# Mixer of a token tower: parameter products woven between the projection jobs, end values turned earlier, B's copies shared differently

## The reference, cut to what matters

```python
proj = x @ w_in
gate, vraw, params = jnp.split(proj, [D_INNER, 2 * D_INNER], axis=-1)
v = jax.nn.silu(conv)                      # causal convolution of vraw over 4 tokens
bc = (v @ w_bc).reshape(Bsz, T, N_HEADS, 2, D_STATE)
Bm = _l2norm(bc[..., 0, :]); Cm = _l2norm(bc[..., 1, :])
A = jax.nn.softplus(p[..., 0]); dt = jax.nn.sigmoid(p[..., 1])
S = 1.0 / (1.0 + dt * dt * A)
...
z = s * (z - d * a * xs + d * bu)          # one token's step, for each head
xs = xs + d * z
y = jnp.einsum('bhn,bhnp->bhp', Ct, xs)
```

## Time and profile before

| what | us |
| --- | --- |
| median of 3 runs | 1756.95 (1753.33 to 1761.33) |
| the profiled execution, its own time | 1750.74 |
| its span from first to last instruction | 1748.9 |
| `mixer_project`, from its first work | 332.3 to 402.3 |
| `mixer_responses` | 402.3 to 449.9 |
| `mixer_bc` | 449.9 to 477.6 |
| `mixer_chain` | 477.6 to 576.9 |

### The profile page before, as it was taken

One profiled execution on the slowest core, in us unless ns is written; L12 is line 12 of the kernel. 1 busy time (PEld: TensorE's weight loads), 2 busy tenths in 40 slices (PEclk: granted clock), 3 DMA queues, 4 the chain that ended last, 5 costly groups with the idle time before them and its releaser, 6 DMA issues. The chain is left out here.

```text
span 1748.9 us, 36641 instructions
## 1 busy us (share of the span) xinstructions
PE 1476.3 (84%) x14396; PEld 1114.7 (64%) x14396; DVE 1280.7 (73%) x2547; ACT 1048.4 (60%) x1871; POOL 414.7 (24%) x424
## 2 busy tenths in 40 slices
PE   5889998798499889899999719995697999999795
PEld 5889897697455657654445618895676744446574
DVE  5988897489789547369995757884655389994566
ACT  6998897334678264548896306664002549995565
POOL 0000000101656120359910117872001310000200
PEclk9999999699599989879999659998797979999897
DMA  5110100100000100025500732121100000000101
GB/s 146 28 42 29 37 1 20 36 1 1 7 2 2 35 1 15 1 82 170 171 16 2 210 119 61 61 62 50 48 1 14 1 1 2 2 2 2 35 1 37
DMA packets 52748, 67.96 MB, mean 39 GB/s; under 512 B 11535, under 2 KB 41489, under 8 KB 52578
## 3 DMA queue, kind: packets, MB, share of 16 engines
q1 hardware_dynamic: 46022, 50.30, 9.6%
q0 software_dynamic: 3840, 9.18, 1.8%
q10 hardware_dynamic: 2716, 6.14, 1.4%
HBM read 46.97 MB, written 18.65 MB: 38 GB/s over the span
## 5 line engine op out<-in xcount | busy, mean ns | idle before, releaser
L2068 DVE TENSOR_REDUCE att_max<-banks 104x1 f32<-104x512 f32 (+1 forms) x480 | 296.8, 684 | 10.2 <-PE banks L1982 6.5
L2103 ACT ACTIVATE att_p<-banks 104x514 f32<-104x514 f32 (+1 forms) x480 | 262.4, 599 | 31.4 <-PE banks L2027 19.1
L339 PE MATMUL banks<-tok_wT,feature_halves 128*128 128x192 f16 x2592 | 228.7, 248 | 23.9 <-DVE feature_halves L365 12.8
L339 PEld LDWEIGHTS banks<-tok_wT,feature_halves 128*128 128x128 f16 x2592 | 216.2, 99 | 33.2 <-DVE feature_halves L365 18.8
L2027 PE MATMUL banks<-att_q,att_kT 64*104 64x257 f16 (+1 forms) x960 | 157.1, 301 | 3.6 <-ACT att_p L2103 2.9
L2043 PE MATMUL banks<-att_p,att_v 104*32 104x257 f32 (+1 forms) x1920 | 154.8, 396 | 0.9
L1982 PE MATMUL banks<-att_kT,att_q 64*104 64x512 f16 (+1 forms) x480 | 126.9, 424 | 5.9 <-DVE att_max L2068 3.5
L2027 PEld LDWEIGHTS banks<-att_q,att_kT 64*104 64x104 f16 (+1 forms) x960 | 62.5, 121 | 107.0 <-ACT att_p L2103 80.4
L365 DVE TENSOR_TENSOR feature_halves<-features,feature_halves 128x2048 f16<-128x2048 f32 x54 | 123.4, 2286 | 6.5 <-ACT feature_halves L462 6.5
L134 PE MATMUL banks<-ones 128*128 128x256 f16 x654 | 88.5, 294 | 27.5 <-PEq L251 13.6
L462 ACT CAST feature_halves<-features 128x2048 f16<-128x2048 f32 x54 | 102.2, 1893 | 10.9 <-PE banks L339 10.1
(11 more groups left out here) (472 smaller groups left out, 3399.0 us busy)
## 6 DMA issues: line engine op xcount, KB each, us to landing
expert_w_in<-in_L_ffn_w_dram SPq DMA_DIRECT2D x16, 576.0 KB, 4.6
expert_w_halves<-expert_w_halves SPq DMA_DIRECT2D x32, 288.0 KB, 2.6
tok_w<-in_L_tok_W_dram ACTq DMA_DIRECT2D x4, 1152.0 KB, 7.2
expert_w2s<-expert_w_halves SPq DMA_DIRECT2D x1, 4608.0 KB
expert_y<-expert_out SPq DMA_DIRECT2D x6, 513.0 KB
expert_w1s<-expert_w_halves SPq DMA_DIRECT2D x2, 1536.0 KB
raw<-in_x_dram SPq DMA_DIRECT2D x2, 1152.0 KB, 5.4
expert_w1s<-expert_w_halves SPq DMA_DIRECT2D x3, 768.0 KB
```

What stands on the lines that cost most here:

```text
L339: ins = pe.matmul(c.bank[t // 2][:, (t % 2) * D:(t % 2 + 1) * D], fh[:, s, q, z, t * 128:(t + 1) * 128], wT[:, y, k, 6 * q + wf, :], start ...
L2068: dve.reduce_max(mx[0:qn, n // NS % 2, 2 * gi + e, k:k + 1], bank_of(unit)[0:qn, 0:KEYS], X).then_inc(maxed, 1)
L2103: act.activation(p[0:kn, n % RING, :, :], c.pair[2 + n % 2][0:kn, :].rearrange("p (e q) -> p e q", e=2)[:, :, 0:HALF], ACT.Exp, scale=scal ...
```

## The change

- In `mixer_project` PE's parameter products no longer stand ahead of the jobs: chunk n's two products are issued ahead of job n, for n up to 35. DVE's first step with the parameters moves to job 38, ACT's three functions to ahead of gate job 41, DVE's lane values to job 54, and PE's eight transposes to behind job 62 (from behind job 36).
- The copies that place the coefficients in the table move from the start of `mixer_responses` to the end of `mixer_project`.
- In `mixer_responses` PE turns the end values ahead of job 20 (a function `ends`), DVE copies them out ahead of the sum of squares, and ACT loads the table of Sqrt at the start with a function of one column.
- In `mixer_bc` the second copy of B's high part is made from the f32 source, one half by DVE (ahead of its wait for ACT's cast) and one by ACT (at its end). DVE subtracts the low part of all columns, POOL none.

The diff, cut to its core:

```diff
@@ mixer_project, tensor
-                for i in range(NBC):
+
+                def params(i):
                     for o in range(2):
                         ins = pe.matmul(c.bank[7][0:L, i * 2 * SH:(i + 1) * 2 * SH],
                                         c.xT[0:DH, o, i * L:(i + 1) * L], w[:, o, 2 * DIN:PROJ],
                                         start=(o == 0), stop=(o == 1))
-                ins.then_inc(pdone, 1)
+                    if i == NBC - 1:
+                        ins.then_inc(pdone, 1)
+
                 for n, (g, m, b, s) in enumerate(jobs):
+                    if n < NBC:
+                        params(n)
                     if n >= 6:
                         pe.wait_ge(ev[n % 2], (n - 6) // 2 + 1)
...
-                    if n == len(jobs) // 2:
+                    if n == NBC + 26:
                         pe.wait_ge(qs, 2)
@@ mixer_project, scalar
+                    if n == NBC + 5:
+                        lanes()
                     if g == 0:
@@ mixer_project, vector
+                    if n == NBC + 2:
+                        dve.wait_ge(pdone, 1)
+                        own.did(dve.tensor_copy(par[0:L, :, :].rearrange("p a b -> p (a b)"),
+                                                c.bank[7][0:L, 0:2 * SH * NBC]))
+                        own.wait()
+                        dve.scalar_tensor_tensor(nega, a, -1.0, a, ALU.mult, ALU.min).then_inc(a2, 1)
+                        own.did(dve.tensor_scalar(tmp[0:L, 3, :], a, 0.0, None, ALU.max))
...
-                    if n == 5:
+                    if n == NBC + 18:
                         dve.wait_ge(a1, 3)
...
+                    if n == len(jobs) - 2:
+                        dve.wait_ge(qt, 1)
+                        own.did(dve.tensor_copy(coef[0:LANES, :, :, :].rearrange("p a b c -> p (a b c)"),
+                                                c.bank[6][0:LANES, 0:8 * L]))
+                        own.wait()
+                        dve.wait_ge(cleared, 1)
...
+                        own.did(dve.tensor_copy(table[:, :, :, 2:2 + (BW - 3) * (BW + 1) + 1:BW + 1], cf[:, 2:4, :, :]))
+                        for z in range(2):
+                            own.did(dve.tensor_copy(table[:, :, :, z], cf[:, 1 - z:3 - z, :, 0]))
@@ mixer_responses, vector
-            own.did(dve.tensor_copy(flat[:, :, :, 2:2 + (SUB - 1) * (BW + 1) + 1:BW + 1], cf[:, 2:4, :, :]))
-            for z in range(2):
-                own.did(dve.tensor_copy(table[:, :, :, 0, z], cf[:, 1 - z:3 - z, :, 0]))
...
-            dve.wait_ge(squares, 1)
+            dve.wait_ge(tail, 1)
+            dve.tensor_copy(ab[0:L, :, :].rearrange("p a b -> p (a b)"), c.bank[6][0:L, 0:4 * P]).then_inc(rest_ev, 1)
+            dve.wait_ge(tail, 2)
+            dve.tensor_copy(zx[0:L, :], c.bank[7][0:L, 0:2 * P]).then_inc(rest_ev, 1)
+            dve.tensor_copy(de[:, :, :].rearrange("p a b -> p (a b)"),
+                            c.bank[7][0:96, 256:256 + 2 * NBC]).then_inc(rest_ev, 1)
+            dve.wait_ge(squares, 2)
@@ mixer_responses, scalar
+            act.activation(ss[:, 0:1], c.ones[0:L, 0:1], ACT.Sqrt).then_inc(squares, 1)
@@ mixer_responses, tensor
+            def ends():
+                pe.wait_ge(moved, 8)
+                pe.wait_ge(joined, 2)
+                pe.wait_ge(placed, 2)
...
+                ins.then_inc(tail, 1)
+                pe.wait_ge(masked, 8)
...
+                ins.then_inc(tail, 1)
             for n, (q, t0) in enumerate(jobs):
                 k = min(4, L - t0)
+                if n == LATE + 2:
+                    ends()
@@ mixer_bc
-            pool.wait_ge(padded, 3)
-            pool.wait_ge(bwh, 1)
-            pool.tensor_tensor(half.wl[0:L, 0:MID], bwf[:, 0:MID], half.wh[0:L, 0:MID], ALU.subtract).then_inc(bwl, 1)
...
+            act.copy(half.wh[64:64 + L, MID:], bwf[:, MID:]).then_inc(again, 1)
...
+            dve.wait_ge(bwd, 2)
+            dve.tensor_copy(half.wh[64:64 + L, 0:MID], bwf[:, 0:MID]).then_inc(again, 1)
             dve.wait_ge(bwh, 1)
             dve.wait_ge(padded, 2)
-            dve.tensor_tensor(half.wl[0:L, MID:], bwf[:, MID:], half.wh[0:L, MID:], ALU.subtract).then_inc(bwl, 1)
-            dve.wait_ge(bwh, 1)
-            dve.tensor_copy(half.wh[64:64 + L, :], half.wh[0:L, :]).then_inc(bwh, 1)
+            dve.tensor_tensor(half.wl[0:L, :], bwf, half.wh[0:L, :], ALU.subtract).then_inc(bwl, 1)
```

More of the change, by code:

```diff
@@ L883, in _, with lanes @@
             def _(act):
[L885 to L889, removed]
+                def lanes():
+                    act.wait_ge(a2, 1)
+                    act.activation(tmp[0:L, 1, :], tmp[0:L, 0, :], ACT.Exp).then_inc(a1, 1)
+                    act.wait_ge(a1, 1)
+                    act.activation(tmp[0:L, 2, :], tmp[0:L, 1, :], ACT.Ln, bias=1.0).then_inc(a1, 1)
+                    act.activation(q3[0:L, 3, :], par[0:L, :, 1], ACT.Sigmoid).then_inc(a1, 1)
                 def silu_u(i):
@@ L996, in mixer_responses @@
     LATE = 18
+    tail = c.sem("resp_tail_turned")
     per = [min(5, NBC - 5 * i) for i in range(8)]
@@ L1110, in _ @@
                 ins.then_inc(done, 1)
+            def ends():
+                pe.wait_ge(moved, 8)
+                pe.wait_ge(joined, 2)
+                pe.wait_ge(placed, 2)
+                for z in range(2):
+                    for q in range(2):
+                        at = (z * 2 + q) * P
+                        ins = pe.transpose(c.bank[6][0:L, at:at + P], g[0:P, q, :, z], idn)
+                ins.then_inc(tail, 1)
+                pe.wait_ge(masked, 8)
+                for q in range(2):
+                    ins = pe.transpose(c.bank[7][0:L, q * P:(q + 1) * P], zend[:, 0, q, 2:W], idn)
+                for j in range(2):
+                    for q in range(2):
+                        at = 256 + j * NBC + q * (NBC // 2)
+                        for z in range(2):
+                            ins = pe.matmul(c.bank[7][0:96, at:at + NBC // 2], c.const(f"sel{z}", P),
+                                            r[0:P, q, (0, 3, 2, 1)[2 * j + z], :], start=(z == 0), stop=(z == 1))
+                ins.then_inc(tail, 1)
             for n, (q, t0) in enumerate(jobs):
                 k = min(4, L - t0)
+                if n == LATE + 2:
+                    ends()
                 if n >= 6:
@@ L1122, in _ @@
                 ins.then_inc(tp, 1)
-            pe.wait_ge(moved, 8)
-            pe.wait_ge(ev, len(jobs))
-            for z in range(2):
-                for q in range(2):
-                    at = (z * 2 + q) * P
-                    ins = pe.transpose(c.bank[6][0:L, at:at + P], g[0:P, q, :, z], idn)
-            ins.then_inc(tp, 1)
-            pe.wait_ge(masked, 8)
-            for q in range(2):
-                ins = pe.transpose(c.bank[7][0:L, q * P:(q + 1) * P], zend[:, 0, q, 2:W], idn)
-            ins.then_inc(tp, 1)
-            for j in range(2):
-                for q in range(2):
-                    at = 256 + j * NBC + q * (NBC // 2)
-                    for z in range(2):
-                        ins = pe.matmul(c.bank[7][0:96, at:at + NBC // 2], c.const(f"sel{z}", P), r[0:P, q, (0, 3, 2, 1)[2 * j + z], :],
-                                        start=(z == 0), stop=(z == 1))
-            ins.then_inc(tp, 1)
 class Halves:
@@ L1156, in mixer_bc @@
     inverse = c.xT[:, 1, NT // 2:NT // 2 + 2 * NG]
-    names = ("zeroed", "padded", "turned", "high", "low", "start_copied", "end_ready", "end_high", "end_low", "normed_ready", "start_ready")
-    zeroed, padded, tp, high, low, acd, bwd, bwh, bwl, nd, acr = (c.sem("bch_" + q) for q in names)
+    names = ("zeroed", "padded", "turned", "high", "low", "start_copied", "end_ready", "end_high", "end_low", "normed_ready", "start_ready", "second_high")
+    zeroed, padded, tp, high, low, acd, bwd, bwh, bwl, nd, acr, again = (c.sem("bch_" + q) for q in names)
     MID = NBC * 96 // 2
```

20 lines of the change are left out of this document (4 added, 16 removed).

## The result

The changed kernel took 1789.4 us (median of 4 runs, 1782.3 to 1793.3), the kernel before 1758.2 (4 runs); the ratio is 1.018, with an interval of 1.014 to 1.021. It is slower, and the forecast of 1747.3 missed by 42 us. The profiled execution took 1791.57, its span is 1789.8.

The account below looks back on a forecast made before the run. DVE was taken to pace stage one and end all three stages, held by POOL's clear in stage two; gains of 1.7 + 6.5 + 1.4 = 9.6 us gave a forecast median of 1747.3, range 1742 to 1754.

Parts of the forecast that it names:

- 3 pairs at half, to 337.7, and 33 at full: Stage one (`mixer_project`): clock rises some 5 us in; the 33 pairs at full clock take 29.4 us, job 35 done at 367.1.
- the clock stays at half through the woven jobs: Rival on stage one, chance 0.08: each pair at half costs 0.89 us more; all 33 add 29, giving 1777.
- The size of a pair: Stage one: parameters and job together take 0.89 us at full clock (0.79 to 1.13), 1.78 at half.
- the two changes between kinds: Stage one: changing from small products to a wide one exposes a weight load, taken as 0.10 us (nothing to 0.15).
- the 1.7: Gain forecast for stage one, in us; bounds a loss of 2 and a gain of 5.
- ACT's detour and the clock behind it: Stage one: waits of 1.0 us (bounds 0 and 2.8) for ACT's table loads, 1.5 (0 and 3.5) for PE's lost clock.
- Stage two: `mixer_responses`: ends with POOL's clear of `acT` at 40.8 us instead of 47.3, a gain of 6.5.
- The cover of the end values: Stage two: DVE's three copies of end values finish within ACT's square's cover, by under 1 us.
- Stage three: `mixer_bc`: ACT's new cast ends it at 475.95 instead of 477.38, gain 1.4 us, bounds 1.0 and 2.0.
- The rivals on POOL's clear: Stage two: scan held by the clear too (chance 0.07, 1753.6), or table copy slow by its form (0.05, 1752.9).
- On transposes: Stage two: the trace shows clock 1.00 on transposes alone; by the skill's contrary rule the sum is 0.9 us smaller.

Follow-up runs that it names:

- weave_late: Changed kernel with chunk n's parameter products ahead of job n + 8, their copy and ACT's lanes eight jobs later too; 1750.9 us, ratio 0.998 to the kernel before.
- weave_warm: Changed kernel with 60 dummy products (128x256) on PE ahead of the first woven pair, nothing else; 1762.0 us, ratio 1.006 to the kernel before.
- blocks6_zero: As blocks6_early, but with the blocks of six chunks' parameter products ahead of jobs 0, 6, ... 30; 1748.6 us, ratio 0.997 to the kernel before.
- lanes_late: Changed kernel with all parameter products ahead of the first job again, the steps behind them left at the change's places; 1751.7 us, ratio 0.999 to the kernel before.
- weave_off: Changed kernel with the parameter products and all steps behind them back where they were, the rest kept; 1746.3 us, ratio 0.996 to the kernel before.
- block12: Changed kernel with all 36 chunks' parameter products in one block behind job 11 and the steps on them moved; 1751.7 us, ratio 0.998 to the kernel before.
- blocks6: Changed kernel with parameter products in blocks of six chunks ahead of jobs 12, 18, ... 42, steps behind them later; 1748.5 us, ratio 0.997 to the kernel before.
- blocks6_split: As blocks6, with ACT's exp, ln and sigmoid placed six jobs apart and the transposes behind job 68; 1745.5 us, ratio 0.993 to the kernel before.
- blocks6_early: As blocks6_split, with everything six jobs earlier, the first block ahead of job 6; 1746.4 us, ratio 0.995 to the kernel before.

## Why the prediction was wrong

**The step that failed** is "3 pairs at half, to 337.7, and 33 at full". None ran at full. The rival with 0.08, "the clock stays at half through the woven jobs", happened. My reason against it, that the wide job had raised the clock before, took a run of nothing but wide jobs for evidence about the same jobs with small products between them. weave_late and weave_warm show that for this mixture the level at the start decides, and blocks6_zero that the grain does. The rival's own time, 1777, was 12 us short of the 1789.4 measured; the next two points account for 10.7 of them.

**The size of a pair** was off too. At half clock 1.93 us was forecast as 1.78, which makes 36 x 0.15 = 5.4 us; with 33 x 0.89 = 29.4 for the clock that is 34.8, and the last pair ended at some 401.6 where I had 367.1, 34.5 later. At full clock 1.09 was forecast as 0.89, inside the bounds of 0.79 to 1.13. In runs of six, a chunk and a job take 0.23 + 0.61 = 0.84, so each pair pays 0.25 for the two changes between kinds; I had 0.10. At half clock it pays 1.93 - 0.40 - 1.16 = 0.37 (blocks6_zero's rows divided by six). With these prices the weave doesn't pay even at full clock: 33 x 0.20 = 6.6 us eat the 1.7. The runs agree: with the steps behind the products late in both, stage one is 74.5 with the weave at full clock (weave_late) and 74.6 with the products up front (lanes_late).

**ACT's detour and the clock behind it** were put at 1.0 and 1.5. From the last pair to the stage's end 38.5 us went by, and 33.2 were forecast: 5.3 over. lanes_late gives 4.5 for the moved steps together, against weave_off. Its two waits, 3.00 and 2.52, come again in the kernel after as 3.07 and 2.51, and there DVE waits 2.35, 1.94 and 1.49 for its three copies behind PE's first: a wait of PE is paid again in the jobs at half clock that follow it.

**Stage two**'s last work, POOL's clear, ended 40.3 us in against 40.8, but for other reasons in part: the table copies alone give 4.1, the early end values (with Sqrt's table) the other 2.8. I had taken the end from POOL's clear and not worked out what the end values would cost if they stayed last; the sum was right because the change moves both. The cover of the end values held, by 1.19 us (DVE's wait ahead of L1090). **Stage three** was right to 0.2 us, and its last work was ACT's. The rivals on POOL's clear fell: the scan ran under it, and the copy took 0.42 without it.

**On transposes** the kernel before shows more than the earlier trace rows. Behind an idle time of 2.98 us PE had nothing but G's transposes from 425.06 on; the clock fell at 426.4 and rose again at 429.8, in the middle of them. PE's timeline, and windows with columns as in the earlier trace rows:

```profile
425.06 8.53 PE L1121 MATMUL banks<-consts,G 108*57 108x108 f32 x72 [2.98 <-DVE G L1033]
```

```profile
428.00:430.00 2.00, 2.00 (x14) 2.00 (x13) 1.87 (x6) 1.58 (x4) 0.07 (x1) 0.54 0.00 0
430.00:432.00 2.00, 2.00 (x24) 2.00 (x23) 2.00 (x2) 2.00 (x5) 0.00 (x0) 1.00 0.00 0
```

Over 461 to 464 in the kernel after, with PE on the same transposes alone, it was 1.00 too. The Trainium skill ("TensorE: Matmul & The Clock Gate", on transpose mode) has it that full clock doesn't engage for them. These traces disagree, for a clock that is up and for one that is down.

**Still open** is what in the alternation keeps the clock at 0.50. PE was busy in all of it, and one dummy a pair didn't change it. The Trainium skill ("TensorE: Matmul & The Clock Gate", Part 1: The HAM clock gate) describes the gate as released by sustained activity of PE. Here PE was busy by the profile for 72 us and the clock stayed at 0.50, so the profile's busy time doesn't tell whether the clock will rise. Which part of a product counts wasn't separated.

## What to carry to other kernels

Work moved between other work on TensorE has two prices: that of changing between the kinds, and that of the clock it finds or leaves. Read the granted clock for the very mixture; if no row has it, start the mixture with the clock up, and weave in groups. ScalarE's detour through table loads stopped nobody at the start of the stage, where PE never waited for ACT; in the middle of the pipeline, with the steps behind it, it cost 4.5 us (lanes_late). Take it apart so that each piece fits into the banks that are full ahead.

## What was not expected of the hardware

- 36 pairs of products at 0.50 for 69.5 us with PE busy throughout, and the same pairs at 1.00 for 39 us after eight jobs or 60 dummies.
- Transposes alone raised the clock from 0.50 to 1.00 (429.8 in the kernel before), which the pairs didn't in 69.5 us.
- A block of small products let the clock fall while PE was busy (block12), blocks of 1.4 us with six jobs between them didn't (blocks6, blocks6_split, blocks6_early, blocks6_zero).
- A change between products of 12 and of 171 columns costs some 0.12 us at full clock, 0.19 at half (by the difference between pairs and runs of six); a dummy of 256 columns put into one is nearly free (0.02 us a pair).
- A copy of 228 columns takes 0.42 us, and 5.94 with POOL's clear beside it; products with two operands run beside the same clear at their usual pace (0.20 us at 440.23).
